# The order of two matmul groups in the even steps of an attention loop

## The chip, the cores and the metric

The kernel runs on one core of a Trainium2 chip. The metric is the device time of one execution in microseconds. PE is the TensorE engine (matmuls), DVE is VectorE, ACT is ScalarE, POOL is GpSimd, SP is SyncE (here it only issues DMAs).

## What is computed

A cross-attention over a context of 1500 rows (a first part of 257 "image" rows, and 1243 "text" rows with weights of their own), and behind it a feed-forward layer with 32 experts. Cut to what matters here:

```
q     = rms_norm(x @ q_w + q_b, nq_s)              # 16 batches x 56 rows, 16 heads x 128
k_txt = rms_norm(txt_ctx @ k_w + k_b, nkt_s);  v_txt = txt_ctx @ v_w + v_b
k_img = rms_norm(img_ctx @ ki_w + ki_b, nki_s); v_img = img_ctx @ vi_w + vi_b
out   = sdpa(q, k_txt, v_txt) + sdpa(q, k_img, v_img)
x     = x + out @ o_w + o_b
x     = x + ffn(layernorm(x))
```

The kernel never forms the keys. The key weights are folded into the queries ahead of the loop (the array u), so that the scores are a product of the context with u. What is still needed of a key is its length, for rms_norm: per context row, one number, got from a product of the context tile with the 256x256 matrix of the key weights (gram) and a sum along the row. The values are not formed either: the loop averages raw context rows by the probabilities, and the value weights are applied at the end.

## The kernel before, in words

The attention loop runs over 16 batches. A batch has 13 tiles of 128 context rows: tiles 0 and 1 of the image part, tile 2 (LONE) which is the image part's last single row, and text tiles 3 to 12. The 16 heads x 56 queries make 896 columns, taken in two halves of 448. A **unit** u is one half of one tile (t = u // 2), so a batch has 26 units, and the code has 26 **steps** per batch.

PE's own order is written out by hand in `body_of(safe).body`. In step s it does, in this order (the safe path, the one that runs):

- `scores(it, s)`: six matmuls of 448 columns (for the lone tile two) into one of three PSUM banks. It waits until DVE has put the seed (a bias) into that bank (`seed`, L1499).
- in four steps per batch `sums` (two matmuls, L1295 and L1296): the denominators, into the bank GRAM. It waits for the norm of the tile before.
- in even steps `gram` of tile s/2 + 1, which may be tile 0 of the next batch: five matmuls of 258 columns (L1231, L1233) into the bank GRAM, the **product** below.
- `average(it, s - 2)`: six matmuls of 448 columns of the context by the probabilities of the unit two back. It waits until DVE has written p_low of that unit (L1488). The lone tile has none. In steps 0 and 1 `carried` averages the last two units of the batch before instead.

Every float32 value is taken apart into a high and a low part, and a product is made of three matmuls, high by high, high by low, low by high.

Around it, in their own orders:

- ACT, for a unit: exp of the scores twice (L1405 into p_high, L1407 back into the bank). It also copies the context tile to its high part (c_high, L1376), and in steps 1 and 2 copies the finished averages of the batch before out of PSUM (`copy_o`, also L1376).
- DVE, in step s (function `take` for unit s - 1): p_low (L1488), the running sum of the probabilities (L1560), the seed of the freed bank (L1499), and in even steps the **norm** (L1513, function `norm`): it multiplies the product in the bank GRAM by c_twice and sums along the row, into key_ms. In steps 2, 4, 8 and 10 (`norms_first`) the norm stands ahead of `take`, otherwise behind it. For the lone tile `take` has an extra part (L1530), and around the last units of the image and text part the sums are split (L1540, L1488).
- POOL, in even steps: the **root** (L1713, key_rms from key_ms, waits for the norm), then in most even steps one large operation for the queries or outputs of a neighbouring batch (L1738, L1763, L1781; 2.1 us). In odd steps the low part of a context tile (c_low, L1719) and then c_twice (L1732), which the next norm reads.

So norm(t) needs product(t) from PE and c_twice(t) from POOL. POOL's c_twice(t + 1) stands in POOL's queue behind root(t), and root(t) waits for norm(t). The function `last_unit_of_buffer`, `P_RING = 3` and the semaphore av_done tie ACT's c_high and p_high to finished averages.

Of the kernel before, what the change touches and what calls it, by code (L numbers as in the profile page):

```python
# [87 lines left out]
def slot(t, ring):  # L88

    return t % ring if t < TILES - 1 else ring  # L90
# [721 lines left out]
def attend(nc, memory, ctx_in, lone_in, qw_in, kw_in, psum, ident, minus_half, zeros, small, key_scale, bias_high, bias_low, x_high,  # L812
# [4 lines left out]
    with ctx:  # L817
# [178 lines left out]
        def ahead(it, t):  # L996
            return (it, t) if t < TILES else (it + 1, t - TILES)
# [218 lines left out]
        def _(pe):  # L1216
# [11 lines left out]
            def gram_products(k, s):  # L1228
                for c in range(NC):
                    for i, part in enumerate((gram_high, gram_low)):  # L1230
                        nc.tensor.matmul(psum[:, GRAM, 0:WB], c_high[:, k, c * P:(c + 1) * P],  # L1231
                                         part[:, s, c, :], start=c == 0 and i == 0, stop=False)
                return nc.tensor.matmul(psum[:, GRAM, 0:WB], lin_pick[:, :], lin_rows[:, s, :], start=False, stop=True)  # L1233

            def gram(it, t):
                pe.wait_ge(ctx_high, TILES * it + t + 1)
                pe.wait_ge(norm_summed, TILES * it + t + CREDIT["norm_summed"])
                gram_products(slot(t, CTX_RING), int(t >= IMG_TILES)).then_inc(gram_done, 1)
# [33 lines left out]
            def average(it, u):  # L1272
                t, half = divmod(u, 2)
                k, n = slot(t, CTX_RING), ROWS[t]
                if t == LONE:
                    return
                pe.wait_ge(probs_split, UNITS * it + u + 1 + CREDIT["probs_split"])
                first, last_tile = t in (0, IMG_TILES), t in (LONE - 1, TILES - 1)
                if t == 0:


                    pe.wait_ge(o_copied, 2 * it + half - 1 + CREDIT["o_copied"])
                for c in range(NC):
                    w = slice(DIM + c * P, DIM + (c + 1) * P)
                    last = three(psum[:, O + 2 * half + c, 0:HALF], c_high[0:n, k, w], c_low[0:n, k, w],
                                 p_high[0:n, probs_slot(u), :], p_low[0:n, probs_slot(u), :], first, last_tile)
                last.then_inc(av_done, 1)

            def sums(it, s, half, grams):

                n = 4 * it + 2 * s + half
                pe.wait_ge(sum_split, n + 1 + CREDIT["sum_split"])
                pe.wait_ge(sum_copied, n + CREDIT["sum_copied"])
                pe.wait_ge(norm_summed, grams + CREDIT["norm_summed"])
                nc.tensor.matmul(psum[:, GRAM, 0:HALF], ones_r[:, :], p_sum_high[:, 2 * s + half, :], start=True, stop=False)  # L1295
                nc.tensor.matmul(psum[:, GRAM, 0:HALF], ones_r[:, :], p_sum_low[:, 2 * s + half, :], start=False, stop=True)\  # L1296
                    .then_inc(sum_wide, 1)

            def carried(it, step):

                if step < 2:
                    average(it - 1, UNITS - 2 + step)

            def text_sums(it, step, grams):
                if step in TEXT_SUMS:
                    sums(it - 1, TEXT, TEXT_SUMS.index(step), grams)

            def sums_left(it, step, has_prev):

                if (has_prev and step - 1 in TEXT_SUMS) or step - 1 in IMAGE_SUMS:  # L1310
                    issued = len([x for x in TEXT_SUMS + IMAGE_SUMS if x < step])
                    pe.wait_ge(sum_copied, 4 * it - 2 + issued + CREDIT["sum_copied"])

            def body_of(safe):
                def body(it, has_prev, has_next):
                    for step in range(UNITS):
                        scores(it, step, safe)
                        grams = TILES * it + step // 2 + 2
                        if has_prev:
                            text_sums(it, step, grams)  # L1320
                        if step in IMAGE_SUMS:
                            sums(it, IMAGE, IMAGE_SUMS.index(step), grams)
                        if step % 2 == 0:
                            sums_left(it, step, has_prev)
                            gram(*ahead(it, step // 2 + 1))
                        if step >= 2:
                            average(it, step - 2)
                        if has_prev:
                            carried(it, step)
                return body  # L1330

            def tail(it):
# [27 lines left out]
            with pe.If(unsafe(pe)):  # L1360
                with pe.Fori(0, B) as it:
                    maxima(it)
                pe.wait_ge(rank_zeroed, 2)
                pe.wait_ge(first_split, 12)
                batches(pe, body_of(False), tail)
            with pe.Else():
                batches(pe, body_of(True), tail)
# [1100 lines left out]
```

## Time and profile before

| | us |
|---|---|
| median of 3 runs (lowest, highest) | 1808.75 (1807.91, 1809.63) |
| the profiled execution | 1808.77 |
| its span, first to last instruction | 1807.0 |
| PE busy | 1718.9 (95%) |
| DVE busy | 1343.6 (74%) |
| POOL busy | 1199.1 (66%) |
| ACT busy | 983.1 (54%) |

The profiled execution is 1.8 us longer than its span. The attention loop is the stretch from 231 us to 1362 us of the span, the projections stand ahead of it, the output product and the experts behind it. A timeline row has the start, the duration (both us), engine, line, operation, out<-in, shapes, count, and in brackets the idle time of the engine before it and what ended it. The end of a matmul is modelled, and consecutive matmuls overlap in the rows, so PE is better read by the distance between starts.

### The profile page before, as it was taken

The page shows a single profiled execution, that of the slowest core. Times are in us where ns is not written, and L with a number is a line of the kernel's source. Part 1 is how long each engine was busy: PE and PEld are TensorE (multiplying, and loading weights), DVE is VectorE, ACT ScalarE, POOL GpSimd, SP SyncE. Part 2 cuts the span into 40 slices and gives each one's busy share as a digit, 9 for nine tenths or more (in the row PEclk, how much of TensorE's full clock was granted, in tenths as well). Part 3 has the DMA queues.
Part 4 walks back from the last instruction along what each step waited for, and adds up shares of the span by engine and source line. Part 5 has one row for each costly group of instructions (what it writes and reads, how often), then busy time and mean ns, then how long its engine had stood idle before and what let it go on. Part 6 is the DMA issues. An engine that isn't in the chain of part 4 may idle for free. (4 is left out here: it accounts for less than half of the span.)

```text
span 1807.0 us, 31191 instructions
## 1 busy us (share of the span) xinstructions
PE 1718.9 (95%) x8731; PEld 1540.5 (85%) x8731; DVE 1343.6 (74%) x2561; ACT 983.1 (54%) x1657; POOL 1199.1 (66%) x1053
## 2 busy tenths in 40 slices
PE   7899989999999999999999999999996997699998
PEld 6677779989889889889899898898885896588887
DVE  4444577887878878878878878778775783677776
ACT  3455546665665665656665656656645662344443
POOL 1233578889888898898898898888866420233332
PEclk8999989999999999999999999999998997899999
DMA  3276574466565665665564665656566960233332
GB/s 116 91 251 230 203 200 109 113 129 125 133 123 123 135 128 119 137 137 124 129 132 120 128 128 131 122 124 134 116 196 185 326 210 28 97 113 114 116 115 71
DMA packets 419413, 251.25 MB, mean 139 GB/s; under 512 B 352320, under 2 KB 370880, under 8 KB 417568
## 3 DMA queue, kind: packets, MB, share of 16 engines
q1 hardware_dynamic: 419360, 250.61, 54.1%
q8 instruction: 26, 0.43, 0.1%
q14 instruction: 27, 0.22, 0.0%
HBM read 187.71 MB, written 60.10 MB: 137 GB/s over the span
## 5 line engine op out<-in xcount | busy, mean ns | idle before, releaser
L1405 ACT ACTIVATE p_high<-psum,key_rms 128x448 fp32r<-128x448 f32 x384 | 245.0, 638 | 345.9 <-PE psum L1226 345.8
L1224 PE MATMUL psum<-u_high,c_high 128*128 128x448 f32 x768 | 284.2, 370 | 6.5 <-POOLq L1837 5.9
L1224 PE MATMUL psum<-p_high,c_high 128*128 128x448 f32 (+1 forms) x768 | 284.8, 371 | 4.9 <-DVE p_low L1488 4.9
L1225 PE MATMUL psum<-u_low,c_high 128*128 128x448 f32 x768 | 281.9, 367 | 0.0
L1226 PE MATMUL psum<-u_high,c_low 128*128 128x448 f32 x768 | 281.6, 367 | 0.0
L1226 PE MATMUL psum<-p_high,c_low 128*128 128x448 f32 (+1 forms) x768 | 280.9, 366 | 0.0
L1225 PE MATMUL psum<-p_low,c_high 128*128 128x448 f32 (+1 forms) x768 | 280.9, 366 | 0.0
L1499 DVE COPY psum<-beta_wide 128x448 f32<-128x448 f32 x416 | 259.3, 627 | 20.2 <-DMA beta_wide<-absorbed_biases 4.4
L1488 DVE TENSOR_TENSOR p_low<-psum,p_high 128x448 fp32r<-128x448 f32 x384 | 236.7, 616 | 45.3 <-ACT psum L1407 42.9
L1719 POOL TENSOR_TENSOR c_low<-stage,c_high 128x512 fp32r<-128x512 f32 x208 | 270.3, 1300 | 0.0
L1407 ACT ACTIVATE psum<-psum,key_rms 128x448 f32<-128x448 f32 x384 | 232.9, 606 | 0.0
L1713 POOL TENSOR_TENSOR key_rms<-key_ms,minus_half 128x1 f32<-128x1 f32 x209 | 120.6, 577 | 132.0 <-DVE key_ms L1513 129.6
L1513 DVE CUSTOM_DVE_ANT_0 junk<-psum,c_twice 128x257 bf16<-128x257 f32 x208 | 88.8, 427 | 136.9 <-POOL c_twice L1732 134.8
L1560 DVE TENSOR_TENSOR p_sum<-psum,p_sum 128x448 f32<-128x448 f32 (+1 forms) x304 | 186.3, 613 | 0.0
L2172 POOL TENSOR_TENSOR scaled_gate<-gated,p_wide 128x448 f32<-128x448 f32 x64 | 83.8, 1309 | 154.1 <-ACT gated L2273 150.4
L1732 POOL TENSOR_TENSOR c_twice<-stage,c_low 128x256 f32<-128x256 f32 x208 | 160.3, 771 | 16.3 <-POOL c_low L1719 2.4
L1224 PEld LDWEIGHTS psum<-u_high,c_high 128*128 128x128 f32 x768 | 145.0, 189 | 25.5 <-DVE psum L1499 7.9
L1224 PEld LDWEIGHTS psum<-p_high,c_high 128*128 128x128 f32 (+1 forms) x768 | 144.0, 188 | 21.5 <-DVE p_low L1488 9.1
L1225 PEld LDWEIGHTS psum<-u_low,c_high 128*128 128x128 f32 x768 | 145.3, 189 | 11.4
L1226 PEld LDWEIGHTS psum<-u_high,c_low 128*128 128x128 f32 x768 | 144.9, 189 | 11.5
L1226 PEld LDWEIGHTS psum<-p_high,c_low 128*128 128x128 f32 (+1 forms) x768 | 144.5, 188 | 11.9
L1225 PEld LDWEIGHTS psum<-p_low,c_high 128*128 128x128 f32 (+1 forms) x768 | 144.9, 189 | 7.8
(274 smaller groups left out, 4032.6 us busy)
## 6 DMA issues: line engine op xcount, KB each, us to landing
stage<-in_ctx SPq DMA_DIRECT2D x210, 256.0 KB, 2.7
averages<-o_raw SPq DMA_DIRECT2D x64, 448.0 KB, 5.2
u_raw<-absorbed_queries SPq DMA_DIRECT2D x60, 448.0 KB, 5.5
absorbed_queries<-u_stage SPq DMA_DIRECT2D x14, 1792.0 KB, 6.8
u_stage<-averages SPq DMA_DIRECT2D x20, 896.0 KB, 6.1
beta_wide<-absorbed_biases SPq DMA_DIRECT2D x32, 448.0 KB, 5.4
recip_wide<-reciprocals SPq DMA_DIRECT2D x32, 448.0 KB, 4.0
p_wide<-probs_by_expert SPq DMA_DIRECT2D x32, 448.0 KB, 3.5
```

What stands on the lines that cost most here:

```text
L1224: nc.tensor.matmul(out, high, rhigh, start=start, stop=False, **kw)
L1225: nc.tensor.matmul(out, high, rlow, start=False, stop=False, **kw)
L1226: return nc.tensor.matmul(out, low, rhigh, start=False, stop=stop, **kw)
L1405: nc.scalar.activation(p_high[:, probs_slot(u), :], src, ACT.Exp, scale=key_rms[:, t:t + 1])
L1407: nc.scalar.activation(out, src, ACT.Exp, scale=key_rms[:, t:t + 1]).then_inc(exp_done, 1)
L1488: return nc.vector.tensor_tensor(out, a, b, ALU.subtract)
L1499: nc.vector.tensor_copy(psum[:, bank_of(u), 0:HALF], beta_wide[:, s, cols_of(half)])\
L1513: nc.vector.tensor_tensor_reduce(out=junk[:, :], in0=psum[:, GRAM, 0:DIM + 1], in1=c_twice[:, slot(t, TWICE_RING), :], scale=1.0 / INNER, ...
L1560: done = nc.vector.tensor_tensor(part if u in IN_BANK else total, part, total, ALU.add)
L1713: nc.gpsimd.tensor_tensor(key_rms[:, t:t + 1], key_ms[:, t:t + 1], minus_half[:, 0:1], ALU.pow)\
L1719: nc.gpsimd.tensor_tensor(c_low[:, k, :], stage[:, st, :], c_high[:, k, :].bitcast(F32), ALU.subtract)\
L1732: nc.gpsimd.tensor_tensor(c_twice[:, slot(t, TWICE_RING), 0:DIM], stage[:, st, nat], c_low[:, k, nat].bitcast(F32), ALU.add).then_inc(stag ...
```

## The change

In PE's order the product and the wait `sums_left` ahead of it move behind the average. Odd steps stay as they were. In step 6 the unit two back is of the lone tile, which has no average, so there nothing moves. No instruction is added or removed.

```diff
@@ body_of(safe), PE
                         if step in IMAGE_SUMS:
                             sums(it, IMAGE, IMAGE_SUMS.index(step), grams)
-                        if step % 2 == 0:
-                            sums_left(it, step, has_prev)
-                            gram(*ahead(it, step // 2 + 1))
                         if step >= 2:
                             average(it, step - 2)
                         if has_prev:
                             carried(it, step)
+                        if step % 2 == 0:
+                            sums_left(it, step, has_prev)
+                            gram(*ahead(it, step // 2 + 1))
```

## Rows read from the trace of the kernel before

**Rows 1.** Windows view: busy us (instructions) of PE, weight loads, DVE, ACT, POOL; clock; DMA.
```profile
900.00:1000.00 100.00, 99.47 (x524) 91.43 (x523) 80.79 (x170) 58.95 (x104) 88.97 (x78) 1.00 0.57 128
```

**Rows 2.** Waits view, 300 to 1300 us, DVE, then POOL: total us, times, longest.
```profile
DVE junk L1513 <- POOL c_twice L1732: 126.1, 125, 1.7
...
POOL key_rms L1713 <- DVE key_ms L1513: 100.9, 157, 0.9
```

**Rows 3.** Timeline, DVE and POOL, 829 to 836 us: norm(7) to norm(8).
```profile
829.98 0.42 DVE L1513 CUSTOM_DVE_ANT_0 junk<-psum,c_twice 128x257 bf16<-128x257 f32 x1
...
830.49 0.69 POOL L1713 TENSOR_TENSOR key_rms<-key_ms,minus_half 128x1 f32<-128x1 f32 x1 [0.83 <-DVE key_ms L1513]
831.15 2.44 POOL L1763 TENSOR_TENSOR u_low<-u_raw,u_high 128x896 fp32r<-128x896 f32 x1
833.55 1.30 POOL L1719 TENSOR_TENSOR c_low<-stage,c_high 128x512 fp32r<-128x512 f32 x1
834.93 0.73 POOL L1732 TENSOR_TENSOR c_twice<-stage,c_low 128x256 f32<-128x256 f32 x1
...
835.69 0.43 DVE L1513 CUSTOM_DVE_ANT_0 junk<-psum,c_twice 128x257 bf16<-128x257 f32 x1 [0.65 <-POOL c_twice L1732]
```

**Rows 4.** Timeline, DVE: norm(2), norm(3), and the next batch's norm(2).
```profile
804.73 0.43 DVE L1513 CUSTOM_DVE_ANT_0 junk<-psum,c_twice 128x257 bf16<-128x257 f32 x1 [0.63 <-POOL c_twice L1732]
...
809.99 0.43 DVE L1513 CUSTOM_DVE_ANT_0 junk<-psum,c_twice 128x257 bf16<-128x257 f32 x1
...
874.97 0.43 DVE L1513 CUSTOM_DVE_ANT_0 junk<-psum,c_twice 128x257 bf16<-128x257 f32 x1 [0.63 <-POOL c_twice L1732]
```

**Rows 5.** Timeline, PE: last matmul of average(2), then scores of unit 5.
```profile
809.17 0.37 PE L1226 MATMUL psum<-p_high,c_low 128*128 128x448 f32 x1
810.09 0.68 PE L1254 MATMUL psum<-x_high,ones_r 128*128 128x448 f32 x2 [0.55 <-DVE psum L1499]
```

**Rows 6.** Timeline, PE: last matmul of product(5), average(6) behind it, product(6), product(7).
```profile
817.20 0.28 PE L1233 MATMUL psum<-lin_rows,lin_pick 128*128 128x258 f32 x1
817.32 0.36 PE L1224 MATMUL psum<-p_high,c_high 128*128 128x448 f32 x1
...
818.55 0.37 PE L1224 MATMUL psum<-u_high,c_high 128*128 128x448 f32 x1
...
823.11 0.28 PE L1233 MATMUL psum<-lin_rows,lin_pick 128*128 128x258 f32 x1
...
829.01 0.28 PE L1233 MATMUL psum<-lin_rows,lin_pick 128*128 128x258 f32 x1
```

**Rows 7.** Timeline, DVE: norm(5) and norm(6) of the same batch.
```profile
818.74 0.43 DVE L1513 CUSTOM_DVE_ANT_0 junk<-psum,c_twice 128x257 bf16<-128x257 f32 x1 [1.02 <-POOL c_twice L1732]
...
824.42 0.42 DVE L1513 CUSTOM_DVE_ANT_0 junk<-psum,c_twice 128x257 bf16<-128x257 f32 x1
```

**Rows 8.** Timeline, last batch: a product's last matmul on PE, its norm on DVE.
```profile
1355.65 0.28 PE L1233 MATMUL psum<-lin_rows,lin_pick 128*128 128x258 f32 x1
...
1355.99 0.43 DVE L1513 CUSTOM_DVE_ANT_0 junk<-psum,c_twice 128x257 bf16<-128x257 f32 x1 [0.74 <-PE psum L1233]
```

**Rows 9.** Timeline, batch 1: last matmul of product(2) on PE, norm(2) on DVE.
```profile
311.88 0.28 PE L1233 MATMUL psum<-lin_rows,lin_pick 128*128 128x258 f32 x1
...
313.11 0.42 DVE L1513 CUSTOM_DVE_ANT_0 junk<-psum,c_twice 128x257 bf16<-128x257 f32 x1
```

**Rows 10.** Timeline: p_low(6) on DVE, the last matmul ahead of product(5) on PE.
```profile
815.91 0.61 DVE L1488 TENSOR_TENSOR p_low<-psum,p_high 128x448 fp32r<-128x448 f32 x1
...
816.51 0.37 PE L1226 MATMUL psum<-u_high,c_low 128*128 128x448 f32 x1
```

**Rows 11.** Timeline, step 1: ACT's copy of the averages, DVE's x_low, POOL's c_twice(2).
```profile
798.94 0.92 ACT L1376 ACTIVATE o_raw<-psum 128x896 f32<-128x896 f32 x1 [2.83 <-PE psum L1226]
...
803.48 0.62 DVE L1488 TENSOR_TENSOR x_low<-p_sum,p_sum_high 128x448 fp32r<-128x448 f32 x1
...
803.50 1.20 POOL L1732 TENSOR_TENSOR c_twice<-stage,c_low 128x256 f32<-128x256 f32 x1
```

## The prediction

> **What bounds the kernel now.** I read the windows of the loop first, then the waits by engine, then the timelines of the waits that the change touches. The windows show a loop at full clock in which PE is 99.5% busy by the rows and POOL 89% [rows 1], which looks like a kernel bound by PE. But the ends of matmuls are modelled and overlap, so gaps below some 0.16 us are not seen there, and starts must be counted instead. Six matmuls of 448 columns take 818.55 - 817.32 = 1.23 us (1.22 in most steps) [rows 6]. A batch has 24 x 6 for scores, 24 x 6 for averages, 4 for the lone tile and 8 for sums, in all 300 at 0.203 = 60.9 us, and 13 products of about 0.60 us, 7.8 us: 68.7 us. The batch lasts 874.97 - 804.73 = 70.24 us, from one norm(2) to the next [rows 4]. So PE waits 1.5 us in each batch. The largest piece is ahead of the scores of unit 5: average(2) is issued out at 809.17 + 0.20 = 809.37, the scores start at 810.09, 0.72 us later, released by DVE's seed [rows 5].
>
> Who sets 70.24 us? The waits say it: from 300 to 1300 us DVE's norm waited for POOL's c_twice 125 times and POOL's root waited for DVE's norm 157 times, in some 185 tiles, while the view has no wait of the norm for PE at all there [rows 2]. The reader is to see a ring: norm(t), root(t), POOL's large operation, c_low, c_twice(t + 1), norm(t + 1). From norm(7) to norm(8) it closes with POOL never idle but for the wait for the norm: 829.98 to 835.69, 5.71 us [rows 3]. Where c_twice is early, DVE takes over without a pause: from norm(2) at 804.73 DVE works through p_low, the sums, and the seeds to norm(3) at 809.99 with no idle time in brackets [rows 4], and the seed of unit 5 lies in this stretch. So the ring of DVE and POOL, 13 links, has the length of the batch, and nothing in it waits for PE. PE is tied to it at the seed of unit 5, and from there runs on its own.
>
> **The change part by part.** Moved: in 12 of 13 even steps the product starts one average later, 1.22 us [rows 6]. The average starts 0.60 us earlier. sums_left moves with the product; the copy it waits for is then older still: nothing. No DMA and no other queue is passed. PE's own sum of work is the same, so on PE alone the cost is 0.
>
> Norm(t) must now wait for the later product where the distance between them was below 1.22 us plus the signal. Where DVE does wait for the product, it starts 1355.99 - (1355.65 + 0.28) = 0.06 us after the modelled end by these rounded rows [rows 8]; I take 0.04 to 0.12. So a norm is pushed if it stood less than 1.26 us behind the modelled end of its product:
>
> - norm(5): 818.74 - (817.20 + 0.28) = 1.26 us: not pushed, or by some hundredths [rows 6, 7].
> - norm(6): 824.42 - (823.11 + 0.28) = 1.03 us: pushed by 0.23 [rows 6, 7].
> - norm(7): 829.98 - (829.01 + 0.28) = 0.69 us: pushed by 0.57 (0.65 with the longer signal) [rows 3, 6].
>
> Product(4) is not moved. PE's position in steps 8 to 12 hangs on the seed of unit 5, so these distances come back in every batch. Norm(7) has the shortest of all 13. Behind norm(7) the ring goes on as before, 0.57 us late: its links are all POOL's or DVE's own work, and the later norms, having stood further behind their products, are not pushed again. It is 0.57 late at norm(2) of the next batch, and so at the seed of unit 5, and PE waits 0.57 us more, most of it at the sums and at average(1), which follow norm(2) in DVE's order. Then PE, 0.57 us later, issues product(5) to (7) relative to that, and the same is pushed again. Each batch becomes 0.57 us longer. What hides the delay elsewhere: c_low, u_low and the lone parts come 1.1 us or more ahead of the scores that read them, so 0.57 fits under them; if it did not, PE would pay the rest.
>
> The sum: batches 2 to 15, 14 passages at 0.57 = 8.0 us. The passage from batch 0 to 1 is another: there norm(2) of batch 1 is 313.11 - (311.88 + 0.28) = 0.95 us behind its product [rows 9], so it is pushed by 1.26 - 0.95 = 0.31 at least and by 1.22 at most (if the products of batch 0 hold the ring all the way); I take 0.8, the middle, for lack of a nearer row. In the last batch the large operations of POOL for a next batch are missing, and PE no longer waits for the ring. Together 8.8 us: 1808.77 + 8.8 = 1817.6 for the profiled execution, and the median is within 0.02 of that one.
>
> Two terms are open. First, average(6) now follows the scores at 816.51 + 0.21 = 816.72, and its p_low is written at 815.91 + 0.61 = 816.52 [rows 10]: 0.20 us of cover. PE's start behind a wait takes about that much where the weights are held up too, so each batch may lose 0 to 0.1 here, straight on the path to product(7): 0 to 1.4 us. I take 0, since the row still shows cover. Second, DVE and POOL hold each other up: c_twice(2) took 1.20 us where c_twice(8) took 0.73, and DVE's x_low started 0.02 us ahead of it [rows 3, 11]. With the ring shifted against ACT and PE such a meeting can come or go: -0.47 to +0.47 us a batch, 7 us either way over 15.
>
> The Trainium skill names this in "SBUF — State Buffer", section "Who interferes with whom": DVE with two SBUF inputs and POOL reading SBUF lock one port pair for a whole instruction, and who issues first wins. The trace agrees with 1.20 against 0.73. By that rule alone the change would move the meeting without removing it, since POOL is nearly always in an operation.
>
> **The rivals.**
>
> *The meeting at c_twice(2) goes away, and the push does not come (faster).* Average(24) of the batch before ends 0.6 us earlier, so ACT's copy at 798.94, which had waited 2.83 us for it, and the exp and p_low behind it come earlier [rows 11]. DVE's x_low at 803.48 then leaves POOL's c_twice(2) alone, and each batch is 0.47 shorter: 15 x 0.47 = 7 us, 1801.7. For it: the copy stands right behind that average. Against it: the x_low waits for its own high part, which met POOL's c_low just before, so DVE would be held there and come out at the same time; and the push by the products must fail as well.
>
> *No difference.* Either the push comes and the meeting goes (0.57 - 0.47 = 0.10 a batch, 1.5 us: 1810), or the ring has slack that the timelines hide. It decides if norm(7)'s delay dies before norm(2): then only 0 to 2 us. Against it: the waits view has the norms waiting for c_twice in most tiles.
>
> *Slower than forecast.* The push comes, average(6) waits 0.1, and new meetings cost 0.3 a batch: 8.8 + 1.4 + 4.5 = 14.7 us, 1823.5.
>
> *It does not do what it says* is no rival: the order on PE is written out, only an idle average (step 6, and steps 0 and 2 of the first batch in part) leaves it unchanged.
>
> **How the numbers follow.** The forecast, 1817.6, has 0.65, with its own range 1813 to 1821 from the meetings at a third of their bound and the first passage. Slower still 0.08. No difference 0.18, at 1806 to 1812. Faster 0.09. About 0.2%, 3.6 us, is what a measurement of this kernel can tell from no change. The forecast and the slower rival lie above 1812.4, the faster one below 1805.1. The range that leaves out no more than 2 in 10 goes from 1807.5, which takes in most of the no-difference case, to 1823.
>
> **What the changed profile would show.** Right: the waits of the loop have a new row, norm for PE's product (L1513 for L1233), once or twice in a batch, about 0.3 us each; norm(7) stands 0.04 to 0.12 us behind the modelled end of its product; norm(2) to norm(2) is 70.8 us; the additional idle time of PE lies ahead of the sums and average(1) in step 3, while scores(5) still wait 0.7 us. Wrong: if norm(7) waits for the product but the batch stays at 70.2 us, the ring was not closed. If c_twice(2) takes 0.73 us, the meeting went. If PE waits ahead of average(6) or (8), the cover there was too thin. If PE's idle time falls anywhere in the batch, an earlier average was worth something that I have put at nothing.

## The result, and the profile after

The changed kernel takes 1821.3 us in the median of 4 runs (1817.77 to 1822.78) against 1809.17 us (1807.91 to 1809.63) for the kernel before: the ratio is 1.0078, with a 95% interval of 1.0061 to 1.0094. The forecast was slower, by 8.8 us; it is slower by 12.1 us.

The profiled execution is the shortest of the four, 1817.77 us with a span of 1816.0, only 9.0 us above the span before. But the loop alone grew by more. The scores of unit 4 start a batch's lone tile; from batch 1 to batch 15 the changed kernel takes 1313.26 - 316.77 = 996.5 us, 71.18 per batch:

```profile
316.77 0.56 PE L1254 MATMUL psum<-x_high,ones_r 128*128 128x448 f32 x2
...
1313.26 0.59 PE L1254 MATMUL psum<-x_high,ones_r 128*128 128x448 f32 x2
```

Before, the same two rows start at 316.05 and 1298.64: 982.6 us, 70.19 per batch. That is 13.9 us in 14 passages, 0.99 us each in the mean, and the passage from batch 0 to 1 adds 0.55. The 14 are not alike: the first (batch 1 to 2) took 69.73 us before, as PE did not have to wait for the seed of unit 5 in batch 1, and 71.19 after, 1.46 more; the other 13 took 70.22 in the mean before and 71.18 after, 0.96 more. So the loop is 14.5 us longer, and in this one execution the part behind it happened to be 5.7 us shorter: from the lone tile of batch 15 to the end it took 508.4 us before and 502.7 after. Below, the length of a batch (14 passages, from the timeline) is the finer measure; the ratio of the runs is the outcome.

The waits view, 300 to 1300 us, first DVE's then POOL's (total us, times, longest), now has the row that the forecast asked for, the norm waiting for PE's product, beside the old ones [rows 2]:

```profile
DVE junk L1513 <- POOL c_twice L1732: 128.0, 109, 2.0
DVE junk L1513 <- PE psum L1233: 33.3, 34, 1.8
...
POOL key_rms L1713 <- DVE key_ms L1513: 114.7, 155, 1.2
```

34 times in 14 batches is more than twice a batch, and 33.3 / 34 = 1.0 us is three times what was forecast for one. One of them is norm(7), as expected. The timeline of PE, then DVE, has product(6), product(7), norm(6) and norm(7) of one batch:

```profile
832.12 0.28 PE L1233 MATMUL psum<-lin_rows,lin_pick 128*128 128x258 f32 x1
...
837.99 0.28 PE L1233 MATMUL psum<-lin_rows,lin_pick 128*128 128x258 f32 x1
...
832.57 0.43 DVE L1513 CUSTOM_DVE_ANT_0 junk<-psum,c_twice 128x257 bf16<-128x257 f32 x1
838.44 0.43 DVE L1513 CUSTOM_DVE_ANT_0 junk<-psum,c_twice 128x257 bf16<-128x257 f32 x1 [0.21 <-PE psum L1233]
```

Both norms start 0.17 us behind the modelled end of their product (832.57 - 832.40, 838.44 - 838.27), where it was 1.03 and 0.69 [rows 3, 6, 7]. The other wait is at the head of the batch. Timeline of the changed kernel, DVE and PE, from norm(0) to norm(2):

```profile
800.85 0.43 DVE L1513 CUSTOM_DVE_ANT_0 junk<-psum,c_twice 128x257 bf16<-128x257 f32 x1 [1.27 <-POOL c_twice L1732]
...
801.20 0.62 DVE L1488 TENSOR_TENSOR p_low<-psum,p_high 128x448 fp32r<-128x448 f32 x1
801.73 0.61 DVE L1560 TENSOR_TENSOR p_sum<-psum,p_sum 128x448 f32<-128x448 f32 x1
802.38 0.63 DVE L1499 COPY psum<-beta_wide 128x448 f32<-128x448 f32 x1
...
803.07 0.48 PE L1224 MATMUL psum<-u_high,c_high 128*128 128x448 f32 x1 [0.66 <-DVE psum L1499]
...
806.10 0.28 PE L1233 MATMUL psum<-lin_rows,lin_pick 128*128 128x258 f32 x1
...
806.55 0.43 DVE L1513 CUSTOM_DVE_ANT_0 junk<-psum,c_twice 128x257 bf16<-128x257 f32 x1 [1.82 <-PE psum L1233]
...
810.22 1.60 DVE L1488 TENSOR_TENSOR x_low<-p_sum,p_sum_high 128x448 fp32r<-128x448 f32 x1
...
812.60 0.43 DVE L1513 CUSTOM_DVE_ANT_0 junk<-psum,c_twice 128x257 bf16<-128x257 f32 x1 [0.77 <-POOL c_twice L1732]
```

Here the reader sees what the forecast had missed. PE stands idle 0.66 us ahead of the scores of unit 0 (803.07), until DVE's seed is done at 802.38 + 0.63 = 803.01. That seed follows norm(0) with no pause: norm, p_low, sum, seed. A batch has 26 units and there are three banks, 26 = 3 x 8 + 2, so units 0 and 1 take the banks of units 24 and 25, only two back, where all others take that of three back. PE is thus tied to the ring a second time, and from there issues product(1) late; norm(1) then waits 1.82 us for it, 0.17 us behind its modelled end where it was 0.94 (798.54 - 797.60 in the same view before).

### The profile page after: what moved, and what is told of

Read it like the earlier page. It is cut to its first block and busy times, and to the rows that moved or that the text cites. A ratio compares the mean times of both kernels' runs of the same rounds, so it can differ in the third digit from the quotient of the medians.

```text
span 1816.0 us, 31191 instructions
## 1 busy us (share of the span) xinstructions
PE 1717.6 (95%) x8731; PEld 1538.9 (85%) x8731; DVE 1348.6 (74%) x2561; ACT 986.6 (54%) x1657; POOL 1195.9 (66%) x1053
## 5 line engine op out<-in xcount | busy, mean ns | idle before, releaser
L1224 PE MATMUL psum<-u_high,c_high 128*128 128x448 f32 x768 | 285.2, 371 | 15.7 <-DVE psum L1499 9.6
L1224 PE MATMUL psum<-p_high,c_high 128*128 128x448 f32 (+1 forms) x768 | 284.5, 370 | 5.0 <-DVE p_low L1488 5.0
L1224 PEld LDWEIGHTS psum<-u_high,c_high 128*128 128x128 f32 x768 | 144.9, 189 | 33.0 <-DVE psum L1499 16.4
L1224 PEld LDWEIGHTS psum<-p_high,c_high 128*128 128x128 f32 (+1 forms) x768 | 144.2, 188 | 27.7 <-DVE p_low L1488 10.2
L1732 POOL TENSOR_TENSOR c_twice<-stage,c_low 128x256 f32<-128x256 f32 x208 | 153.6, 739 | 16.4 <-POOL c_low L1719 2.4
```

The source lines that it names most:

```text
L1224: nc.tensor.matmul(out, high, rhigh, start=start, stop=False, **kw)
L1732: nc.gpsimd.tensor_tensor(c_twice[:, slot(t, TWICE_RING), 0:DIM], stage[:, st, nat], c_low[:, k, nat].bitcast(F32), ALU.add).then_inc(stag ...
```

## Where the ring is held: one step at a time

The theory after the result, "two gates": the ring of DVE and POOL sets the batch; PE hangs on it at the seeds of units 0 and 5; in each of the two stretches between, the norm that is pushed furthest counts. Its push is 1.22 us (the average) and 0.16 us (the signal), less its distance from its product before. For the first stretch that is norm(7), for the second norm(1). The rivals: norm(7) alone, with the rest from meetings of DVE and POOL; and a cost of the earlier average itself.

The edit of the next five kernels is the same, with a set of steps. Each batch length below is the mean of the 14 passages in one profile, with its difference to the 70.19 us before; "run" is the ratio to the kernel before, timed again beside it, with its 95% interval.

```diff
-                        if step % 2 == 0:
+                        if step % 2 == 0 and step not in LATE:
                             sums_left(it, step, has_prev)
                             gram(*ahead(it, step // 2 + 1))
                         ... average, carried ...
+                        if step in LATE:
+                            sums_left(it, step, has_prev)
+                            gram(*ahead(it, step // 2 + 1))
```

**LATE = (12,), product(7) alone.**

> Only step 12 (product(7)) moves behind its average, all other steps as before. Theory 'two gates': norm(7) is pushed by 0.65 us, the passage from batch to batch grows from 70.19 to 70.8 us, and the run by 14 x 0.65 = 9 us; norm(1) stands 1.6 us behind its product's modelled end or, if PE is held back at the scores of unit 0 as well, 0.95 as before. Rival 'one gate and meetings' (my forecast): also 9 us here. Rival 'an earlier average costs': under 3 us, since only one average is moved.

Measured: batch 70.79 us, +0.60; run 1.0070 (1.0045 to 1.0094). As all theories but the last say. What tells more is norm(1): in the mean of 14 batches it stands 0.88 us behind its product (0.89 before), though the ring is late, so PE was held back too, at unit 0. The waits view of this kernel, PE, 300 to 1300 us, shows where, at the first scores of the batch (L1224) beside those of unit 5 (L1254):

```profile
PE psum L1224 <- DVE psum L1502: 9.4, 14, 0.8
PE psum L1254 <- DVE psum L1502: 6.8, 13, 0.5
```

In the same view of the kernel before, only the second is listed:

```profile
PE psum L1254 <- DVE psum L1499: 6.9, 13, 0.6
```

**LATE = (0,), product(1) alone.**

> Only step 0 (product(1)) moves. Theory 'two gates': norm(1) stood 0.95 us behind its product, needs 1.22 + 0.16 = 1.38, so it is pushed by 0.43 us a batch, 14 x 0.43 = 6 us. Rival 'one gate and meetings': norm(7) alone matters, 0 us here (within 2).

Measured: batch 70.50 us, +0.32; run 1.0054 (1.0033 to 1.0075). Not 0 as in my forecast, and less than the 0.43 of the theory. The timeline of DVE shows where the rest went (medians of 14 batches): from norm(0) to norm(1) it is 5.69 us instead of 5.26, the 0.43 of the theory, but from norm(1) to norm(2) it is 6.06 instead of 6.18. There POOL's c_twice(2) now takes 0.73 us instead of 1.20. So the push comes in full, and a meeting of DVE and POOL that goes away gives 0.12 back.

**LATE = (0, 12).**

> Steps 0 and 12 move, no other. Theory 'two gates': the same as the full change, 0.95 to 1.0 us a batch, 13 to 14 us in all, because PE is held back a second time at the scores of unit 0 and so meets the ring anew at product(1). Rival 'one gate and meetings': 0.65 us a batch, 9 us, and the missing 0.3 us only in the full change.

Measured: batch 71.22 us, +1.03; run 1.0086 (1.0067 to 1.0106). Two steps of thirteen give all of the change (+0.99). Norm to norm, each push has the size that it has alone: 0.44 from norm(0) to norm(1), 0.61 from norm(6) to norm(7) (0.63 alone). The batch lengths of the parts sum to 0.92; the 0.1 us between is not explained by these runs.

**LATE = (2, 4, 22, 24), the norms that stood far behind.**

> Steps 2, 4, 22 and 24 move, whose norms stood 1.45 to 1.67 us behind their products, over 1.38. Theory 'two gates': 0 us (within 1.5), every norm where it was. Rival 'an earlier average costs or gives something' (the average of step 2 and 4 stands close behind its p_low): 1 to 4 us to either side.

Measured: batch 70.22 us, +0.04; run 1.0014 (1.0002 to 1.0026). In the 13 usual passages the difference is 0.00 us, as expected; the 0.04 comes from the first alone (70.26 against 69.73). Norm(2) came to stand 0.45 us behind its product where it was 1.66, and the ring did not move. So in a usual batch these four earlier averages neither cost nor give. The runs' interval, 0.4 to 4.7 us slower, lies just above zero and doesn't exclude the rival's 1 to 4 us; the profile, of the shortest of the ten runs, shows no such cost in the loop but 0.5 us in the first passage and 0.26 in the one before it.

**LATE = all even steps but 0, 6 and 12.**

> All products move but those of steps 0 and 12. Theory 'a norm is pushed by 1.38 us less its distance from its product, and the largest push of the stretch counts': norm(10) stood 0.92 behind, 0.46 us a batch, 14 x 0.46 = 6.4 us (5 to 7). A theory in which only steps 0 and 12 cost: 0 us. A theory in which every push adds: norm(6) 0.30 + norm(8) 0.41 + norm(9) 0.26 + norm(10) 0.46 + norm(11) 0.13 = 1.6 us a batch, 22 us.

Measured: batch 70.60 us, +0.42; run 1.0034 (1.0019 to 1.0049). The rule of the largest push holds (0.46 expected). Norms 5, 6, 8 and 10 all stand 0.16 to 0.17 us behind their products now, so four are pushed and the batch pays about for one: the pushes don't add, nor are steps 0 and 12 the only ones that can cost. With those two put back, norm(10) is next.

## Is it the ring?

**One operation more on POOL.**

```diff
                     if step % 2 == 0:
                         key_root(*ahead(it, step // 2 + 1))
+                        if step == 16:
+                            nc.gpsimd.tensor_tensor(spare[:, 0:1], minus_half[:, 0:1], minus_half[:, 0:1], ALU.pow)
```

> Order as before; one more root-sized operation on POOL in step 16 of each batch, on a column that nobody reads. Theory (closed ring): each batch grows by what the operation takes, 0.55 to 0.65 us, 8 to 9 us in all, though POOL is 89% busy and off PE's direct path. Rival (PE sets the batch): 0 us.

The operation's own row, by its tile (ns in the shortest, the median and the longest of 16):

```profile
L1792 POOL TENSOR_TENSOR spare<-minus_half x16: 552/552/553, 284.8 to 1346.1; 128x1 f32<-128x1 f32 x16
```

Measured: batch 70.67 us, +0.48; run 1.0052 (1.0034 to 1.0069). An operation that PE never sees, on an engine that is busy 89% of the time, lengthens the batch by 88% of itself, and all of it between norm(9) and norm(10), where it stands (5.78 us instead of 5.27). PE, busy 99.5% by its rows, was not the bound.

**One operation less.** This kernel leaves a part of its output unscaled.

```diff
+                if s == 0 and half == 1:
+                    at = at[:, :, 0:28]
+                    ... the same multiplication, on these 28 columns ...
+                    return
```

> Order as before; in step 22 POOL scales 28 of the 448 columns of the second image half instead of all (this part of the output is left unscaled), 2.13 us become 0.2 to 0.3. Theory (closed ring): the batch falls by 1.2 to 1.5 us, down to PE's own work or to the next wait of a norm for its product, 17 to 22 us in all. Rival (PE sets the batch): 0 us.

Measured: batch 69.20 us, -0.99; run 0.9919 (0.9900 to 0.9938). The waits ahead of the scores of unit 0 and of unit 5 are both gone: by the starts of PE's matmuls the second was 0.69 us long and is 0.00 now. Less than 1.2: norm(0) and norm(1) now stand 0.17 us behind their products, so PE's products are the next bound there even without the change.

**POOL's idle time taken out of the ring.** POOL waits 0.55 us or more for most norms with its large operation still to do. The root moves behind that operation:

```diff
-                    if step % 2 == 0:
-                        key_root(*ahead(it, step // 2 + 1))
-                    else:
+                    if step % 2 == 1:
                         split_tile(*ahead(it, step // 2 + PREP))
                         twice(*ahead(it, step // 2 + PREP))
                     ... the large operations ...
+                    if step % 2 == 0:
+                        key_root(*ahead(it, step // 2 + 1))
```

> Order on PE as before; on POOL the root moves behind the large operation of its step, so that POOL no longer idles 0.55 us per tile for the norm. Theory (the ring of DVE and POOL sets the batch, PE has 1.5 us of waiting in it): the batch falls towards PE's own work, 68.7 to 69.2 us, and the run gets 15 to 22 us faster, about 1790. Rival (PE or the seeds set the batch): no change; or slower, where the exp waits for its later key_rms (the exp of an even unit started 3.9 us after root(7) began; the root would be 1.6 us later).

Measured: batch 69.91 us, -0.27; run 0.9967 (0.9956 to 0.9977). Faster, but by a third of what I expected in the run (6.0 of 15 to 22 us), and by about a fifth in the batch. The ring is off: c_twice is ready 1.4 to 3.4 us ahead of most norms (not of norms 5 to 7, with 0.03 to 0.9), and norms 0, 1 and 9 to 12 stand at their products, 0.16 to 0.17 us behind. Something else took over within 0.3 us. Timeline of this kernel, DVE, step 1 to norm(2):

```profile
796.91 0.62 DVE L1488 TENSOR_TENSOR x_low<-p_sum,p_sum_high 128x448 fp32r<-128x448 f32 x1
799.27 0.62 DVE L1488 TENSOR_TENSOR p_low<-psum,p_high 128x448 fp32r<-128x448 f32 x1 [1.74 <-ACT psum L1407]
...
801.00 1.57 DVE L1540 CAST p_sum_high<-p_sum 128x448 fp32r<-128x448 f32 x1
802.60 0.63 DVE L1488 TENSOR_TENSOR x_low<-p_sum,p_sum_high 128x448 fp32r<-128x448 f32 x1
803.14 0.42 DVE L1513 CUSTOM_DVE_ANT_0 junk<-psum,c_twice 128x257 bf16<-128x257 f32 x1
```

Norm(2) waits for nobody but DVE itself: DVE idles 1.74 us for the exp of unit 0, and then a cast that takes 0.39 us elsewhere takes 1.57, while POOL's u_low runs from 800.19 to 802.31; it ends 0.26 us behind it. That u_low is the cause is read from the overlap, not tried.

**The same with the change.**

> The kernel with the change, and POOL's root behind the large operation. Theory: with the ring off the path the later product costs nothing: within 3 us of the kernel that has only the root moved, near 1790. Rival (the moved product or the earlier average costs PE something of its own): 8 to 13 us slower than that kernel.

Measured: batch 70.57 us; run 1.0037 (1.0023 to 1.0051). The move still costs 0.65 us a batch. My expectation failed. The norms waited for PE 128 times now, and product(1) has a way to the scores of unit 5 that doesn't pass POOL: norm(1), and behind it, in DVE's own order, all that stands up to the seed. PE's rows bear it out. From the last matmul of product(1) to the scores of unit 5 it was 12.81 us with the root alone moved, and it is 12.03 now (medians of 14). So product(1) had 0.78 us of slack there, the other 0.44 of its 1.22 us are paid, and 0.22 more are lost around the scores of unit 0: 0.66, the measured 0.65.

**ACT's order as well.** In steps 1 and 2 the exp moves in front of the copy of the finished averages:

```diff
-                    if has_prev:
+                    if has_prev and step == 0:
                         carried(it, step)
                     if step >= 1:
                         exponentials(it, step - 1)
+                    if has_prev and step >= 1:
+                        carried(it, step)
```

> Products in front as before; POOL's root behind the large operation, and on ACT the exp of steps 1 and 2 in front of the copy of the finished averages. Theory (with the root moved, norm(2) is held by DVE's own order: DVE idles 1.7 us for the exp of unit 0, which stands on ACT behind the copy that waits for average(24)): norm(2) starts at its product, 1.3 to 1.5 us earlier, the batch falls from 69.9 to 68.7 to 69.0 us, the run to about 1785 to 1790, 1% under before. Rival (the wait ahead of norm(2) is the port meeting with POOL alone): within 3 us of the kernel with only the root moved, 1800.

Measured: 1787.3 us (1786.36 to 1788.88) against 1805.85, ratio 0.9895 (0.9880 to 0.9909); batch 69.10 us. This is the fastest kernel of the study, 1.05% under the kernel before. Counted as in the prediction, against 68.7 us of PE's own work, PE's wait falls from 1.5 to 0.4 us a batch. The windows view has PE at 99.98 of 100 us where it was 99.47 [rows 1]:

```profile
900.00:1000.00 100.00, 99.98 (x531) 92.78 (x531) 84.36 (x169) 60.07 (x105) 91.07 (x79) 1.00 0.63 128
```

**ACT's order alone, on the kernel before.**

> Only ACT's order changes, root and products as before. Theory (norm(2) is held by POOL's c_twice(2) in the ring): 0 us, within 2, whatever DVE gains. If the meeting of x_low and c_twice(2) (1.20 against 0.73 us) goes away with DVE's earlier start: down to 0.47 us a batch, 7 us faster. This is the faster rival of my forecast, tried alone.

Measured: batch 70.06 us, -0.13; run 1.0001 (0.9987 to 1.0016). Alone it gives nothing: norm(2) is still held by c_twice(2). The meeting did leave c_twice(2), which takes 0.74 us here instead of 1.20:

```profile
801.54 0.74 POOL L1734 TENSOR_TENSOR c_twice<-stage,c_low 128x256 f32<-128x256 f32 x1
```

but only 0.13 of the 0.46 us reached the batch. So the mechanism of my faster rival exists and is worth a quarter of its price. As the run with step 0 alone showed, it also came with the change, and took 0.12 us a batch off its cost.

**Both orders, with the change.**

> The same two edits on the kernel with the change (every product behind its average). Theory 'the product's place costs only through norms that gate something': with slack ahead of norm(2) the cost shrinks from 0.65 us a batch to 0 to 0.3, 0 to 4 us over the kernel without the move. Rival 'the moved product costs in itself': 8 to 10 us over it.

Measured: batch 70.92 us; run 1.0028 (1.0015 to 1.0041). The move now costs 1.82 us a batch in the mean, and by the medians the run is 24 us over the kernel without it (1811.16 - 1787.3), against 0 to 4 expected: the largest miss. Timeline of this kernel, PE and DVE, from product(1) to the scores of unit 5:

```profile
802.29 0.28 PE L1233 MATMUL psum<-lin_rows,lin_pick 128*128 128x258 f32 x1
...
809.45 0.48 PE L1295 MATMUL psum<-p_sum_high,ones_r 128*128 128x448 f32 x1 [0.19 <-DVE key_ms L1515]
...
806.63 2.42 DVE L1490 TENSOR_TENSOR x_low<-p_sum,p_sum_high 128x448 fp32r<-128x448 f32 x1
808.98 0.42 DVE L1515 CUSTOM_DVE_ANT_0 junk<-psum,c_twice 128x257 bf16<-128x257 f32 x1
...
814.32 0.68 PE L1254 MATMUL psum<-x_high,ones_r 128*128 128x448 f32 x2 [0.52 <-DVE psum L1501]
```

and of the kernel with both orders and no move, from product(1) to the same place:

```profile
789.85 0.28 PE L1233 MATMUL psum<-lin_rows,lin_pick 128*128 128x258 f32 x1
...
794.19 2.43 DVE L1490 TENSOR_TENSOR x_low<-p_sum,p_sum_high 128x448 fp32r<-128x448 f32 x1
796.54 0.41 DVE L1515 CUSTOM_DVE_ANT_0 junk<-psum,c_twice 128x257 bf16<-128x257 f32 x1
...
801.88 0.68 PE L1254 MATMUL psum<-x_high,ones_r 128*128 128x448 f32 x2
```

From product(1) to the scores of unit 5 it is 12.03 us in both (814.32 - 802.29, 801.88 - 789.85). That stretch is DVE's, norm(1) to the seed of unit 5, and in the faster kernel it is just as long as PE's own work beside it. Once that is so, product(1) has no slack at all, and moving it by one average costs the full 1.22 us. With 0.22 us around the scores of unit 0 that makes 1.44.

This is what ten of the 14 batches show: they last 70.5 us, 1.4 more than the 69.1 without the move. The mean of 1.82 comes from the other four, of 71.65, 71.65, 72.01 and 72.22 us. In these four PE stands 0.8 us at the sums of step 11 (L1295), waiting for a norm, and in the ten it doesn't. What tips a batch into this was not tried.

## Why the prediction was right and wrong

- **PE waits 1.5 us a batch for a closed ring of DVE and POOL.** Right: 0.552 us on POOL gave 0.48, and 1.8 us taken from it (2.13 to 0.31) gave 0.99 back. The busy shares alone would have said the opposite.
- **The product of step 12 pushes norm(7).** Right, and alone it costs 0.60 us against 0.57 forecast. Its parts were both a little off. The signal was read in the wrong place: in batches 1 to 14 a norm that waits for its product starts 0.16 to 0.17 us behind the modelled end, and most of those in batches 0 and 15 start 0.04 behind. I took 0.04 to 0.12 from a row of the last batch [rows 8]. And some of the push is lost on the way. In the full change three norms share it: the ring falls behind by 0.10 us up to norm(5), 0.22 more at norm(6) and 0.32 more at norm(7), 0.64 in all (norm to norm, medians of 14 batches).
- **"PE is tied to it at the seed of unit 5, and from there runs on its own."** This is the step that failed. PE hangs on the ring also at the seed of unit 0. The rows were there to be read. Timeline of the kernel before, PE, then DVE, around the first scores of a batch:

```profile
795.15 0.37 PE L1226 MATMUL psum<-p_high,c_low 128*128 128x448 f32 x1
795.52 0.47 PE L1224 MATMUL psum<-u_high,c_high 128*128 128x448 f32 x1
...
794.84 0.63 DVE L1499 COPY psum<-beta_wide 128x448 f32<-128x448 f32 x1
```

The scores start 0.37 us behind the last matmul of average(23), where 0.20 is usual, and DVE's seed had ended at 795.47. The prediction named only the largest piece of PE's 1.5 us and passed over this one of 0.12 to 0.26. It is not the cost of going round the loop: in the two kernels with the root behind and the products unmoved, and in the one with an operation less, the same distance is 0.20 to 0.21 in every batch. With PE tied there, the ring's delay no longer helps norm(1) to stay clear of product(1), and "are not pushed again" is untrue for it: it is pushed by 0.43 us, of which 0.12 come back at c_twice(2). Step 0 alone (+0.32) and steps 0 and 12 together (+1.03) show it.

- **The passage from batch 0 to 1** was put at 0.8 and measured 0.55, within its bounds of 0.31 and 1.22. The passage from batch 1 to 2 was priced like all others, 0.57, and cost 1.46: in batch 1 PE had not been waiting for the seed of unit 5 before.
- **Average(6) with 0.20 us of cover.** Right at 0: in the changed kernel no wait appears ahead of it, and its p_low ends 0.14 us before it starts. The 0.20 us that the prediction gives a start behind a wait are about right as a sum: PE starts 0.05 to 0.06 us behind the end of the seed of unit 5, and its next matmul comes 0.10 late.
- **The meeting of DVE and POOL at c_twice(2).** It changed sides: c_twice(2) takes 0.73 us in the changed kernel, and DVE's x_low 1.60 instead of 0.62, now beside POOL's c_low (809.90 to 811.34). Norm(1) to norm(2) became 6.05 us where it was 6.19 (804.73 - 798.54), 0.14 less, inside the bound of 0.47.
- **Where PE's new idle time lies.** The forecast put it ahead of the sums and average(1) of step 3. By PE's starts, 0.65 of the 0.96 us lie ahead of the scores of unit 0, and the other 0.3 at the sums and the average of step 3.
- **The sum.** 8.0 us for 14 passages should have been 13.9. The push per batch, put at 0.57, measured 0.96 in 13 of them (5.0 us too little), and the first was 0.9 more than its 0.57; the passage from batch 0 to 1 was 0.25 less. The direction held. The 9.0 us of the profiled execution look like the forecast of 8.8 only by accident: the part behind the loop was 5.7 us shorter in it.

## What to carry to other kernels

When every engine is below 100% and each waits a little for the next, look for a closed ring, and test it by adding a small known operation to the engine that nobody suspects. Read the length of every passage and not only the mean: here one passage of 14, and in another kernel four, were of a different kind. Moving work on another engine is free only up to the distance between its end and its reader, at each of the places where the two meet, and the places where the mover itself is held back by the ring divide the loop into stretches, each with a price of its own. A gap of 0.17 us in a dense stream of matmuls was such a place here, where 26 units share three banks.

## What the runs showed of the hardware

From the lone tile of batch 15 to the end the fourteen profiles of this study took 501.4 to 509.1 us, and from the last average of the loop to the end, where no edit reaches, 439.9 to 445.8 us. The granted clock is part of it: in the windows view, 1500 to 1600 us of the span, it was 0.81 in the kernel before and 0.85 in the changed one, and the same at equal places of the code, so the time at the lower level, 1.2 GHz, was longer in the one. One profile therefore can't tell differences below some 6 to 8 us of the whole span; the length of a batch can, as 13 of the 14 lie within 70.12 to 70.24 us before and all 14 within 71.13 to 71.23 after.

A meeting of DVE and POOL can make an operation last longer than either does by itself: in the kernel with both orders and the change, x_low, 0.62 us by itself, took 2.42 us beside POOL's u_low of 2.28 us, which had started 0.34 us before it. By the Trainium skill ("SBUF — State Buffer", "Who interferes with whom") an operation of DVE with two SBUF inputs that comes second waits for the whole of a POOL instruction that reads SBUF; the trace agrees with 2.42 us, and with x_low ending 0.48 us behind u_low's end.
